# Graph attention with LayerNorm on one core: a tile's matmuls in three blocks, P's transfers on one queue, another order of the last tiles

## What is computed

```python
scale = d ** (-0.5)
q = (x @ Wq).reshape(h, n, d)
k = (x @ Wk).reshape(h, n, d)
v = (x @ Wv).reshape(h, n, d)
a = jnp.einsum('hnd,hmd->hnm', q, k) * scale
a = a + adj + adj
mask = adj == 0.0
a = jnp.where(mask, -1000000.0, a)
a = jax.nn.softmax(a, axis=-1)
a = jnp.where(mask, 0.0, a)
out = jnp.einsum('hnm,hmd->hnd', a, v)
out = out.transpose(1, 0, 2).reshape(n, h * d)
y = x + out @ Wout
result = (y - mean(y)) / sqrt(var(y) + 1e-5)     # over each row
```

## Time and profile before

| | |
|---|---|
| time, median of 3 runs | 1842.18 us |
| the profiled execution: its own time / its span from first to last instruction | 1842.29 us / 1840.6 us |
| TensorE matmuls busy | 1807.2 us, 98% |
| TensorE weight loads busy | 1580.4 us, 86% |
| VectorE / ScalarE / GpSimd busy | 1114.2 / 849.4 / 985.0 us |
| granted TensorE clock, mean | 0.996 of full |

### The profile page before, as it was taken

One profiled execution on the slowest core, in us unless ns is written; L12 is line 12 of the kernel. 1 busy time (PEld: TensorE's weight loads), 2 busy tenths in 40 slices (PEclk: granted clock), 3 DMA queues, 4 the chain that ended last, 5 costly groups with the idle time before them and its releaser, 6 DMA issues.

```text
span 1840.6 us, 29367 instructions
## 1 busy us (share of the span) xinstructions
PE 1807.2 (98%) x10272; PEld 1580.4 (86%) x10272; DVE 1114.2 (61%) x2316; ACT 849.4 (46%) x1411; POOL 985.0 (54%) x764
## 2 busy tenths in 40 slices
PE   8999899999999999999999999999999999999997
PEld 7887789888898888988888888888888888898886
DVE  6898855556555565555555655556555555555666
ACT  5654544444544445444454435444454444453432
POOL 7888754444544456444564445544454444654443
PEclk9999999999999999999999999999999999999999
DMA  7888864666646666466664666556665566655664
GB/s 251 247 254 275 254 200 145 195 191 197 189 135 199 185 198 185 139 195 188 193 184 149 193 188 193 169 155 196 196 188 162 169 188 191 196 164 156 178 178 111
DMA packets 187027, 345.97 MB, mean 188 GB/s; under 512 B 39424, under 2 KB 96768, under 8 KB 170496
## 3 DMA queue, kind: packets, MB, share of 16 engines
q10 hardware_dynamic: 92224, 200.85, 34.8%
q1 hardware_dynamic: 94656, 143.24, 28.1%
HBM read 190.84 MB, written 18.87 MB: 114 GB/s over the span
## 4 chain that ended last, share of the span: by engine, by line
PE 86%; DVE 1%; SPq 0%; ACTq 0%; issue 0%; POOL 0%; DMA 0%; POOLq 0%; ACT 0%; DVEq 0%
PE bank L398 34%; PE y_bank L421 22%; PE bank L363 17%; PE y_bank L419 12%; PE y_bank L417 1%; SPq L302 0%; ACTq L567 0%; DVE blocks L654 0%; POOL p_split L472 0%; DMA p_turned<-blocks 0%; PE bank L383 0%; POOLq L254 0%; DVE y_acc L677 0%; DVE y_acc L674 0%; DVE ln L714 0%
## 5 line engine op out<-in xcount | busy, mean ns | idle before, releaser
L472 POOL TENSOR_TENSOR p_split<-p_turned,p_split 128x512 fp32r<-128x512 f32 x512 | 651.8, 1303 | 619.3 <-ACT p_split L539 619.1
L398 PE MATMUL bank<-k_split,q_split 128*128 128x512 f32 x3072 | 787.4, 392 | 0.0
L421 PE MATMUL y_bank<-v_split,p_split 128*128 128x512 f32 x1920 | 701.8, 399 | 0.0
L398 PEld LDWEIGHTS bank<-k_split,q_split 128*128 128x128 f32 x3072 | 576.2, 188 | 110.0
L631 DVE CUSTOM_DVE_ANT_0 t_p<-bank,m_sb 128x512 f32<-128x512 f32 x512 | 351.3, 687 | 365.7 <-PE bank L398 343.6
L419 PE MATMUL y_bank<-v_split,p_split 128*128 128x256 f32 x2048 | 555.8, 282 | 0.0
L530 ACT ACTIVATE t_p<-t_p,small 128x2048 f32<-128x2048 f32 x128 | 256.8, 2006 | 432.5 <-DVE small L643 423.5
L421 PEld LDWEIGHTS y_bank<-v_split,p_split 128*128 128x128 f32 x1920 | 362.6, 189 | 76.4
L419 PEld LDWEIGHTS y_bank<-v_split,p_split 128*128 128x128 f32 x2048 | 389.3, 190 | 18.3
L461 POOL TENSOR_TENSOR w_slot<-raw_w,w_slot 128x512 fp32r<-128x512 f32 x192 | 250.1, 1305 | 196.1 <-ACT w_slot L510 193.7
L654 DVE STREAM_TRANSPOSE blocks<-t_p 128x2048 f32<-128x2048 f32 x128 | 295.9, 2312 | 78.7 <-ACT t_p L530 66.7
(11 more groups left out here) (45 smaller groups left out, 712.7 us busy)
## 6 DMA issues: line engine op xcount, KB each, us to landing
m_sb<-m_dram ACTq DMA_DIRECT2D x112, 1024.0 KB, 5.2
p_turned<-blocks SPq DMA_DIRECT2D x1528, 64.0 KB, 2.1
p_turned<-blocks ACTq DMA_DIRECT2D x520, 64.0 KB, 2.6
blocks<-in_adj_dram SPq DMA_DIRECT2D x64, 256.0 KB, 3.9
raw_w<-in_L_gnn_Wv_dram ACTq DMA_DIRECT2D x64, 256.0 KB, 3.5
m_dram<-m_sb SPq DMA_DIRECT2D x16, 1024.0 KB, 6.4
raw_w<-in_L_gnn_Wq_dram ACTq DMA_DIRECT2D x63, 256.0 KB, 3.4
raw_w<-in_L_gnn_Wk_dram ACTq DMA_DIRECT2D x61, 256.0 KB, 3.9
```

Source lines behind the costliest of these rows:

```text
L398: mm = nc.tensor.matmul(dst[:], q[:, a, k, f * P:(f + 1) * P], k_split[:, kk, k, b * BANK:(b + 1) * BANK], start=(i == 0), stop=(i == len( ...
L421: mm = nc.tensor.matmul(y[:], hi, v_split[:, j].rearrange("p s d -> p (s d)"), start=False, stop=last)
L472: nc.gpsimd.tensor_tensor(lo, p_turned[:, i * BANK:(i + 1) * BANK].rearrange("p (j b) -> p j b", b=QUAD), hi.bitcast(F32), ALU.subtract).t ...
```

## The change

1. **Whole tiles.** For head 1 on, except tile 15 of the heads 1 to 6, TensorE does 24 score matmuls, then all 16 high matmuls of the values, then the 16 low ones, then the projections that are due. These are named under a new place in `due`, `BEHIND_VALUES` (4), which every engine handles after its loop over the banks. Some projections are moved in time for this: q from bank 1, vt 0 and 1, v 0 to 2 and vt 2 to 4, the transposition of x and the first q of the next head now come behind the values of their tile; tile 3 keeps eight between its banks. Tile 0 keeps key chunk 7 behind its first bank.
2. **By bank.** Head 0 and tile 15 of the heads 1 to 6 keep a quarter of the values behind each bank, but now ahead of the projections, and with four high matmuls followed by four low ones.
3. **Transfers.** From tile 16 to tile 126 SP issues all 16 transfers of a tile. The function `shuffle` of ScalarE is still called, and with no transfer of its own it still waits for the transposition of the tile and for the low part of the one before.
4. **Places.** Tile 14 is the first that may be transposed into `blocks[1]`, instead of tile 17, so that tiles 14 to 16 need not wait for the transfers of the tile just before.
5. **Exponential.** ScalarE's `exp_tile(tau)` stands at the end of the loop over the banks and ahead of the `BEHIND_VALUES` keys, instead of at the start of the next iteration.
6. **The end.** LayerNorm's parts become 12, 2 and 2 tiles; the first part's variance, root and inverse come earlier; the last tile is transposed ahead of `add_y`; VectorE makes two of the last tile's four low parts; the stores become four larger and two single ones.

```diff
+        ONE_PLACE = TILES - 2
+
         adj_place = [blocks[1][:, i * BANK:(i + 1) * BANK] for i in range(BANKS)]
 
         def turned_place(tau):
-            return blocks[0 if tau <= TILES else tau % 2]
+            return blocks[(tau - ONE_PLACE + 1) % 2 if tau >= ONE_PLACE else 0]
 
         def turned_before(tau):
-            return tau - 1 if tau <= TILES else tau - 2 if tau > TILES + 1 else None
+            return tau - 1 if tau < ONE_PLACE else tau - 2 if tau > ONE_PLACE else None
...
-        LATER_V = {(1, 3): (("vt", 0),), (2, 0): (("vt", 1),), (2, 1): (("v", 0), ("vt", 2), ("v", 1), ("vt", 3)),
-                   (2, 2): (("v", 2), ("vt", 4)), (2, 3): (("v", 3), ("vt", 5)), (3, 0): (("v", 4), ("vt", 6)),
-                   (3, 1): (("v", 5), ("vt", 7)), (3, 2): (("v", 6), ("v", 7))}
+        BEHIND_VALUES = BANKS
+        LATER_V = {(1, BEHIND_VALUES): (("vt", 0), ("vt", 1)),
+                   (2, BEHIND_VALUES): (("v", 0), ("vt", 2), ("v", 1), ("vt", 3), ("v", 2), ("vt", 4)),
+                   (3, 0): (("v", 3), ("vt", 5)), (3, 1): (("v", 4), ("vt", 6)), (3, 2): (("v", 5), ("vt", 7)),
+                   (3, 3): (("v", 6), ("v", 7))}
...
+        def by_bank(tau):
+            h, t = divmod(tau, TILES)
+            return h == 0 or t == TILES - 1 and h + 1 < H
...
-            if t % 2 == 0 and t <= LAST_Q and b == (2 if tau == 0 else 1):
+            if t % 2 == 0 and t <= LAST_Q and b == (BEHIND_VALUES if h else 2 if t == 0 else 1):
                 yield "q", h, t // 2 + 1
...
-                if (t, b) == (TURN_X, 3):
+                if (t, b) == (TURN_X, BEHIND_VALUES if h else 3):
                     yield "x", h + 1
-                if (t, b) == (TILES - 2, 2):
+                if (t, b) == (TILES - 2, BEHIND_VALUES if h else 2):
                     yield "q", h + 1, 0
...
+            for key in due(tau, BEHIND_VALUES):
+                in_order(key)
         w_keys = list(w_order)
         W_FROM = {"k": wk, "q": wq, "vt": wv}
-        LAST_TILES = ALL - 2
-        EARLY_NORM = TILES - 3
-        NORM_PARTS = [slice(0, EARLY_NORM), slice(EARLY_NORM, TILES - 1), slice(TILES - 1, TILES)]
-        EARLY_OUT = EARLY_NORM // 2 * 2
+        EARLY_NORM = TILES - 4
+        NORM_PARTS = [slice(0, EARLY_NORM), slice(EARLY_NORM, TILES - 2), slice(TILES - 2, TILES)]
+        FIRST_NORM = slice(0, 3)
...
-            return QUADS - 1 if tau < LAST_TILES else QUADS // 2
+            return QUADS - 1 if tau < TILES else QUADS if tau < ALL - 1 else QUADS // 2
...
-                sp.wait_ge(normed, 8)
-                store_out(0, 4)
                 sp.wait_ge(normed, EARLY_NORM)
-                store_out(4, EARLY_OUT // 2)
-                for t in range(EARLY_OUT, TILES):
+                store_out(0, EARLY_NORM // HALVES)
+                sp.wait_ge(normed, TILES - 2)
+                store_out(EARLY_NORM // HALVES, C - 1)
+                for t in range(TILES - 2, TILES):
                     sp.wait_ge(normed, t + 1)
                     sp.dma_start(out_tokens[t % 2][:, t // 2], y_tokens[:, t % 2, t // 2]).then_inc(stored, 16)
-                sp.wait_ge(stored, 16 * (2 * HALVES + TILES - EARLY_OUT))
+                sp.wait_ge(stored, 16 * 3 * HALVES)
...
-                def values(tau, g):
+                def values(tau, first, stop):
                     h, t = divmod(tau, TILES)
                     y = y_bank[tau % 2]
-                    if g == 0:
+                    if first == 0:
                         pe.wait_ge(p_lo, 4 * (tau + 1))
                         if tau >= 2:
                             pe.wait_ge(y_added, tau - 1)
-                    if t == 0:
-                        wait_emptied(("v", h, 2 * g))
-                        wait_emptied(("v", h, 2 * g + 1))
-                    for j in range(TPB * g, TPB * (g + 1)):
-                        hi, lo = (p_split[tau % 2][:, part, j * P:(j + 1) * P] for part in (HI, LO))
-                        first, last = j == 0, j == CHUNKS - 1
-                        if first:
-                            nc.tensor.matmul(y[:], hi, v_split[:, j].rearrange("p s d -> p (s d)"),
-                                             start=True, stop=False)
-                        nc.tensor.matmul(y[:, 0:D], lo, v_split[:, j, HI], start=False, stop=False)
-                        if not first:
-                            mm = nc.tensor.matmul(y[:], hi, v_split[:, j].rearrange("p s d -> p (s d)"),
-                                                  start=False, stop=last)
-                    if g == BANKS - 1:
+                    for j in range(first, stop):
+                        if t == 0 and j % HALVES == 0:
+                            wait_emptied(("v", h, j // HALVES))
+                        nc.tensor.matmul(y[:], p_split[tau % 2][:, HI, j * P:(j + 1) * P],
+                                         v_split[:, j].rearrange("p s d -> p (s d)"), start=(j == 0), stop=False)
+                    for j in range(first, stop):
+                        mm = nc.tensor.matmul(y[:, 0:D], p_split[tau % 2][:, LO, j * P:(j + 1) * P],
+                                              v_split[:, j, HI], start=False, stop=(j == CHUNKS - 1))
+                    if stop == CHUNKS:
                         mm.then_inc(y_done, 1)
+
+                def project_due(tau, b):
+                    for key in due(tau, b):
+                        if key[0] == "x":
+                            turn_x(key[1])
+                        elif key[0] == "v":
+                            project_v(key)
+                        else:
+                            project_x(key)
 
                 pe.wait_ge(ident_ready, 1)
                 turn_x(0)
                 for key in START:
                     project_x(key)
                 for tau in range(ALL + LAG):
-                    for g in range(BANKS):
+                    for b in range(BANKS):
                         if tau < ALL:
-                            scores(tau, g)
-                        for key in due(tau, g):
-                            if key[0] == "x":
-                                turn_x(key[1])
-                            elif key[0] == "v":
-                                project_v(key)
-                            else:
-                                project_x(key)
-                        if LAG <= tau < LAST_TILES or tau >= ALL:
-                            values(tau - LAG, g)
-                    if LAST_TILES <= tau < ALL:
-                        for g in range(BANKS):
-                            values(tau - LAG, g)
+                            scores(tau, b)
+                        if tau >= LAG and by_bank(tau):
+                            values(tau - LAG, b * TPB, (b + 1) * TPB)
+                        project_due(tau, b)
+                    if tau >= LAG and not by_bank(tau):
+                        values(tau - LAG, 0, CHUNKS)
+                    project_due(tau, BEHIND_VALUES)
...
                             lo_p(tau - 2, 2 * b)
-                            lo_p(tau - 2, 2 * b + 1)
+                            if tau < ALL + 1:
+                                lo_p(tau - 2, 2 * b + 1)
                         if tau + 1 < TILES and b:
...
-                    if 1 <= tau <= ALL:
-                        exp_tile(tau - 1)
                     if TILES <= tau + 1 < ALL:
...
+                        split_due(tau, b)
+                        if tau == ALL and b == 1:
+                            sqrt_of(0, NORM_PARTS[0])
                         if 1 <= tau <= ALL and b == 2:
                             for i in range(QUADS):
                                 shuffle(tau - 1, i)
                         if t == 0 and tau < ALL and b == (1 if tau == 0 else BANKS - 1):
                             hi_wout(h)
-                    if tau == ALL:
-                        sqrt_of(0, NORM_PARTS[0])
+                    if tau < ALL:
+                        exp_tile(tau)
+                    split_due(tau, BEHIND_VALUES)
...
+                def lo_p(tau, i):
+                    hi, lo = (by_chunk(p_split[tau % 2][:, part])[:, :, i, :] for part in (HI, LO))
+                    dve.wait_ge(p_hi, 4 * tau + i + 1)
+                    nc.vector.tensor_tensor(lo, p_turned[:, i * BANK:(i + 1) * BANK].rearrange(
+                        "p (j b) -> p j b", b=QUAD), hi.bitcast(F32), ALU.subtract).then_inc(p_lo, 1)
...
+                    if tau == ALL:
+                        turn(tau - 1)
                     if tau > LAG:
                         add_y(tau - LAG - 1)
                         if tau - LAG - 1 >= (H - 1) * TILES:
                             moments((tau - LAG - 1) % TILES)
                     if tau + 1 < TILES:
                         build(t + 1, 0)
-                    if 1 <= tau <= ALL:
+                    if 1 <= tau < ALL:
...
+                    for key in due(tau, BEHIND_VALUES):
+                        lo_of(key)
```

(11 more changed lines are left out.)

20 lines of the change are left out of this document (12 added, 8 removed).

## The result

The changed kernel takes 1877.1 us (median of six runs, 1868.2 to 1884.2) against 1842.1 before: **slower by 1.9%, ratio 1.019, interval 1.0162 to 1.0218**. The forecast of 1841.6 was 35.5 us too low, and the result lies outside its range of 1827 to 1850. The profiled execution took 1875.4 us with a span of 1873.7, which is 33.1 above the span before.

What follows compares the result with a forecast made beforehand. TensorE's matmuls were taken to bound the kernel, busy throughout nearly all of heads 1 to 7. From 1842.3 us: minus 12.0 (whole tiles), plus 14.7 (head starts), minus 1.4 (head 0), minus 2.0 (end) gives 1841.6, range 1827 to 1850.

Steps and rivals of the forecast that it cites:

- Transfers on SP: nothing: SP issuing sixteen transfers a tile takes 10.1 us; late landings stay hidden before the values, so no time is lost.
- elsewhere I find the keys in time: Apart from the wait at a head's first tile, projected keys and weights were claimed to arrive without delaying TensorE.
- Rival C: SP becomes the bound if an issue takes over 0.73 us; at 0.80, 1850 us in all; chance 0.08.
- The wait at a head's start: TensorE waits 2.1 us before bank 3 of tile 0 for key chunk 7, seven times: plus 14.7 us, bounds 10 to 23.
- Rival B: No wait at the head's start, because a chained step comes 2 us earlier: 1826.9 us; chance 0.18.
- The lower clock behind a wait: At the end, a 4.1 us wait had cost TensorE its full clock; whether a shorter one would was left open.
- the sign of being right: A head of 225.1 us was listed among the observations that would show the forecast right.
- Whole tiles: Grouping scores, high and low matmuls saves 0.11 us a tile, 1.65 a head: minus 12.0 us, bounds 0 and 27.
- Rival D: Regrouped matmuls cost what they did, a pair's 0.353 us being no matter of order: 1853.6 us; chance 0.06.
- The new end: After the last scores, tile 127's values begin at 25.9 to 27.7 us: minus 2.0, between plus 0.5 and minus 4.
- the split of low parts: At the end, VectorE and GpSimd sharing tile 127's low parts need 3.8 to 4.4 us to the values, against 5.75.
- Head 0: In its last tile a quarter of values fills the 1.39 us wait for key chunk 1: minus 1.4, bounds 0 and 6.4.

Runs made afterwards that it cites:

- experiment 4: The kernel before, with SP issuing all 16 transfers of a tile from tile 16 to 125, nothing else changed: 1842.6 us, ratio 1.001.
- experiment 2: The changed kernel with one transfer of each quarter back on ScalarE's queue up to tile 126, tile 0 whole: 1861.8 us, ratio 1.0117.
- 1: The changed kernel with tile 0 of heads 1 to 7 done by bank, SP still issuing all transfers: 1845.5 us, ratio 1.0025.
- experiment 3: The changed kernel with both tile 0 by bank and one transfer of each quarter back on ScalarE's queue: 1828.8 us, ratio 0.9936.
- experiment 9: The kernel of experiment 3 with the 1 MB mask load issued behind the fourth high part of P, not ahead of the first: 1822.5 us, ratio 0.9894.
- experiment 11: The changed kernel with only the mask load moved behind the fourth high part of P: 1854.8 us, ratio 1.0069.
- experiment 12: The changed kernel with tile 0 by bank and the mask load moved behind the high parts, SP issuing all transfers: 1824.4 us, ratio 0.9911.
- experiment 7: The kernel of experiment 3 with high and low matmuls of the values alternating again: 1837.7 us, ratio 0.9977.
- experiment 8: The kernel of experiment 3 with the old places for the transposed blocks (second buffer from tile 17, not 14): 1830.6 us, ratio 0.994.

## Why the prediction was wrong

**The step that failed is "Transfers on SP: nothing".** Its rate was right: SP issues one every 0.63 us. What failed were two sentences. One took the landing as 2.1 us from the median of the earlier trace rows, though a mask load is in flight for 5.2 us of every tile (median, kernel before). In the kernel after, transfers issued during one land after 3.7 us at the median and up to 8.1. The other was "elsewhere I find the keys in time". I followed a late transfer only to the exponential and the values, and there the margin did hold (experiment 4, and the whole tiles of every trace). I did not ask what else ScalarE has in its queue behind a waiting high part. In tile 15 these are the high parts of keys and weights, with GpSimd's splits and TensorE's projections behind them. Predicted 0; shown: 15.3 and 16.7 us (the change against experiment 2, and 1 against 3). The term was wrong together with one I had not written at all, the mask load in the new order: some 6 us of the same waits stay with ScalarE's share (experiment 3 against 9). Together they are the 21 to 22 us of experiments 11 and 12 against the change and 1, of which 16.8 in the change are the waits themselves. Rival C had the right queue and the wrong mechanism: SP never became the bound (experiment 12), and at 0.63 us an issue its sixteen fit into every tile.

**The wait at a head's start** was right in place, number and chain, and wrong in size: 3.3 us for 2.1, seven times. The stated upper bound of 3.3, a GpSimd split in the way of a small VectorE instruction, was what happened, each time. I took the short length because the trace of before has it at every head start, and did not see that the same split started 0.06 us behind it there. That it went well before was as near a thing as that it went badly after. Rival B, no wait, falls.

**The lower clock behind a wait was not priced.** I named it for the end alone. It cost some 10 us in heads 1 to 7, and a wait of 3.29 us costs 4.6 on average (experiment 11: (226.12 x 2 + 227.73 x 3 + 228.89) / 6 - 222.83 = 4.6), and tile 0 whole 30 to 33 us in all and not 14.7. Heads came to 228.2 to 234.0 us, where 225.1 was the sign of being right.

**Right.** Whole tiles: predicted 1.65 us for a head, measured 1.77 (224.60 to 222.83, with 14 whole tiles and not 15, since tile 0 is by bank there). Rival D falls with experiment 7: alternating again costs 1.50 us in the tiles 0 to 14, 7.6 to 8.9 in all. So the order of high and low is not indifferent, as the rule of the Trainium skill named in the prediction ("TensorE: Matmul & The Clock Gate", "Back-to-back issue gap") would have it; a pair costs 0.353 us in alternation and 0.346 (5.54 / 16) out of it. The section gives its formula for a single matmul by itself, and says that in a stream with weight loads both operations set the spacing; that the neighbour makes no difference was my reading of it. The new end: tile 127's values began 26.8 us behind the last scores, inside the 25.9 to 27.7 forecast, and the end is 1.5 us shorter (2.0 forecast). With ScalarE sharing tile 126's transfers it is 36.5 us (experiments 3 and 9), and 39.6 to 41.8 with SP alone (1, 12). In the split of low parts the sum held by luck (4.3 us from high part to values, 3.8 to 4.4 forecast): a low part on VectorE took 1.52 us beside GpSimd's, outside the 0.67 to 1.25 that I gave it.

**Open.** Head 0 came out 4.3 us shorter (1.4 forecast), but its length varies from 228.3 to 232.4 us between traces of kernels with the same order in it. Which edit, if any, shortened it isn't settled; experiment 8 speaks against the places of the transposed blocks. What in the new order takes the cover away from tile 15, the values ahead of the projections there or ScalarE's exponential in its new place, no run separates. Why one wait of 3.3 us is followed by a stretch at the lower clock and the next is not, I haven't tried to find.

## What to carry to other kernels

When a transfer gets later, follow the engine that waits for it, and price everything that stands behind that wait in its queue in the busiest tile, not only the consumer of the data. Take a landing time from the transfers that fly with the big load, not from the median of all, and put the big load where it delays what nobody wants yet: here one moved issue was worth 21 us with all transfers on one queue, and 6 with a quarter of them on the other. And where a wait on TensorE is new, add the lower clock behind it to its price.

## What the runs showed that I had not expected

- A VectorE instruction on 128x1 elements (L680) can be held by GpSimd. Of its 128 executions in the kernel after, the 38 that began with no GpSimd split in flight took 0.214 to 0.218 us every time; the 90 that began during one took between 0.214 and 1.36. Its mean rose from 0.371 to 0.642 us (groups of the kernel before, then after). The Trainium skill, "SBUF — State Buffer", section "SBUF: two separate sides", says that VectorE, with two inputs in SBUF, and GpSimd share a pair of ports that the first to start holds for its whole instruction, the other being blocked. The trace agrees on the blocking: at 715.62 in the fence above, L680 ends with GpSimd's L471 (716.95 and 716.94), 1.33 us for 0.21 of work. It doesn't show who was first, since L680's row starts 0.05 us ahead of L471's.

```profile
L661 DVE SCALAR_TENSOR_TENSOR small<-small 128x1 f32<-128x1 f32 x128 | 47.5, 371 | 0.0
```

```profile
L680 DVE SCALAR_TENSOR_TENSOR small<-small 128x1 f32<-128x1 f32 x128 | 82.2, 642 | 0.0
```

- Transfers of 64 KB within SBUF land after 2.0 us at the median when no mask load is in flight, and after 3.7 when issued during one, with a longest of 8.1 (kernel after). The 1 MB load itself takes 6.1 us at the median and up to 9.7.
- The changed kernel's time spreads by 0.9% (1868 to 1884), that of the kernel of experiment 9 by 0.05% (four runs). Why isn't shown; no run was made for it.
